# Router logits with the tokens' columns on the loaded side of TensorE, and VectorE reading them out of PSUM

## The chip, the cores and the metric

The kernel is one program on 1 core of one Trainium2 chip. The metric is the device time of the program in microseconds (us), as the median of repeated runs. The document also shows one profiled execution of the kernel, taken by the hardware profiler.

## The reference: what is computed

A transformer block over 4 sequences of 2048 tokens of width 256 (8192 tokens in all): a modulated layer norm, causal linear attention with 16 heads of width 16 and its output product, a gated residual sum, a second modulated layer norm, and a mixture of experts with 8 experts, of which each token takes 2. The part that the change touches is the router:

```python
logits = xf.astype(jnp.float32) @ w_router.T        # [8192, 256] @ [256, 8]
gates = jax.nn.softmax(logits, axis=-1)
topk_gates, topk_idx = jax.lax.top_k(gates, TOP_K)  # TOP_K = 2
expert_mask = jax.nn.one_hot(topk_idx, N_EXPERTS, dtype=jnp.int32).sum(axis=1)
position_in_expert = jnp.cumsum(expert_mask, axis=0) - 1
```

Everything is float32. The tokens' places with their experts come from a running count over all tokens, so group follows group in the routing.

## The kernel before, in words

The kernel has an attention phase and an expert phase. The attention phase goes over 64 tiles of 128 tokens, written as slots n. Four tiles make a group (16 groups), and q = n % 4 is the place of a slot in its group. In each slot every engine issues its own list of instructions in a fixed order, and the engines meet through semaphores. The loop is unrolled by 8 slots, so there are even groups (slots 0 to 3 of the eight) and odd groups (slots 4 to 7).

What stands in a slot on PE (TensorE), in its order: the scores of the tile (`scores`, L1269), which VectorE (DVE) then multiplies by the causal mask in two instructions (L919); what belongs to the next group's projections (`stage1_qk`, L1365, in q = 1 and 2; `stage1_v`, L1375, in q = 3; `stage1_transposes`, L1349, in q = 0); the transpositions of the tile before (`head_rows`, L1279); the products with the state (L1289, after the first half of DVE's mask) and the key rows (`key_rows`, L1295, after the second half); products within the tile (L1305); the transposed attention rows (L1330, after DVE's `An`, L935); the state (L1320, and L1315 in slot 0 of the eight alone); the output product (L1338); and last, in q = 0, the router's logits of the group two before (`logits`, L1417).

`stage1_qk` with m = 0, in q = 1, splits the activations into a high and a low part. Its last two matmuls wait for the low part `hT`, which GpSimd (POOL) makes in two instructions (L532) after ScalarE (ACT) has made the high part (L656); both of these hang on the transpositions of q = 0 (L1349) and not on the logits.

The logits now: `w_r` (256 x 32, of which 8 columns count) is the loaded side of PE, in two chunks `cc`, and the 128 token columns of `h2T` stream past it, once for each of the 4 tiles t. The four tiles go to four different bands of 32 output partitions of PJ[1] (`PJ[1][32 * t:32 * t + 32, 0:P]`). So the logits stand with the experts on the partitions. In the next slot (q = 1) ACT copies them to SBUF (`lgT`, L732), PE transposes them after its scores (`logit_rows`, L1424), ACT copies the result to `lg` (`take`, L699), after the masked queries for the next tile (L709), and DVE starts the routing (`choose`): `lmax` (L985) and `lp` (L987) are its first two steps, set between the small instructions ahead of `An`. In the tail, slot 63 has the logits of group 14 and slot 68 those of group 15.

The routing ends in q = 3 with L1053 (semaphore `route`), and GpSimd then sends the rows of the group to their experts with 8 indirect DMAs (L495). The expert phase begins when all rows are sent.

Of the kernel before, what the change touches and what calls it, by code (L numbers as in the profile page):

```python
# [17 lines left out]
ALU = mybir.AluOpType  # L18
ACT = mybir.ActivationFunctionType
AX_X = mybir.AxisListType.X  # L20

P = 128
D = 256
DC = D // P
# [10 lines left out]
GT = 4  # L35
# [3 lines left out]
E = 8  # L39
# [10 lines left out]
NR = 28  # L50


def adaln_block(nc, x, wqkv, wo, wr, wg, wd, c, wmod, out, xe, mod_rows):
    with ExitStack() as ctx:
        def sb(name, shape, dt=F32):
            return ctx.enter_context(nc.sbuf_tensor(name, shape, dt))

        def ps(name):
            return ctx.enter_context(nc.psum_tensor(name, [P, 512], F32))

        def sem(name):
            return ctx.enter_context(nc.semaphore(name))
# [11 lines left out]
        h2T = sb("h2T", [P, DC, GW])  # L74
# [7 lines left out]
        w_qkv = sb("w_qkv", [P, 2, DC, 3 * D], F32R)  # L82
        w_o = sb("w_o", [P, DC, D])
        w_r = sb("w_r", [P, DC, 32])
        lgT = sb("lgT", [P, P])
        w_g = sb("w_g", [P, 2, DC, F], F32R)
        cT = sb("cT", [P, DC, BATCH])
        cS = sb("cS", [P, DC, BATCH])
# [3 lines left out]
        ident = sb("ident", [P, P])  # L92
# [24 lines left out]
        nb2 = sb("nb2", [P, GT])  # L117
        den = sb("den", [P, H])
        rden = sb("rden", [P, H])
        lg = sb("lg", [P, GT, E])  # L120
        lmax = sb("lmax", [P, GT])
        lp = sb("lp", [P, GT, E])
        lp2 = sb("lp2", [P, GT, E])
# [8 lines left out]
        pick = sb("pick", [P, 2, GT, E])  # L132
# [46 lines left out]
        PJ = [ps("PJ0"), ps("PJ1")]  # L179
# [7 lines left out]
        lg_ps = PJ[1][:, P:2 * P].rearrange("p (t w) -> p t w", t=GT)  # L187
# [61 lines left out]
        h2t_full = sem("h2t_full")  # L249
        h2t_done = sem("h2t_done")  # L250
        wr_zero = sem("wr_zero")
        lgt_full = sem("lgt_full")
        lgt_done = sem("lgt_done")
        lg_full = sem("lg_full")
        taken = sem("taken")
        route = sem("route")
        gexp = sem("gexp")
        numbered = sem("numbered")
# [38 lines left out]
        def tile_ok(n):  # L297
            return 0 <= n < TILES
# [8 lines left out]
        def group_ok(n):  # L307
            return 0 <= n < GROUPS
# [310 lines left out]
        def _(act):  # L619
# [73 lines left out]
                for t in range(GT):  # L693
                    normalise(N1[:, t, :], t, L * GT + t, rs1, nb1, n1_ready)

            def take(dst, src, s_full, g):

                act.wait_ge(s_full, g + 1)
                act.activation(dst[:], src, ACT.Copy).then_inc(taken, 1)  # L699

            def next_tile_queries(T, q, gp, tp, n):

                q1, g1 = (q + 1) % 4, (gp if q < 3 else 1 - gp)
# [17 lines left out]
            def slot_(it, j, n):  # L721
                T = it * 8 + j
                G = it * 2 + j // 4
# [3 lines left out]
                stage1 = group_ok(nx)  # L727
                g, step = routing(n)
                routed = group_ok(g)
                if routed and step in ("first", "pick"):  # L730
                    act.wait_ge(lgt_full, g + 1)
                    act.activation(lgT[:], PJ[1][:, 0:P], ACT.Copy).then_inc(lgt_done, 1)  # L732
                if tile_ok(n + 1) and q != 3:
                    next_tile_queries(T, q, gp, tp, n)
                if routed and step in ("first", "pick"):
                    take(lg, lg_ps[:, :, 0:E], lg_full, g)
                def columns_out():
                    for cidx in range(DC):
                        act.wait_ge(h2t_full, 2 * g + cidx + 1)
# [73 lines left out]

            act.wait_ge(dve_setup, 2)
            run_slots(slot_, early)


# [51 lines left out]
        def _(dve):  # L869
# [102 lines left out]
            def wide(a):  # L972
                return a.unsqueeze(2).to_broadcast([P, GT, E])

            def done(ins):
                ins.then_inc(route, 1)

            def choose(g, k):

                if k == 0:  # L980
                    dve.wait_ge(taken, g + 1)
                else:
                    dve.wait_ge(route, NR * g + k)
                if k == 0:
                    done(dve.tensor_reduce(lmax[:], lg[:], AX_X, ALU.max))  # L985
                elif k == 1:
                    done(dve.tensor_tensor(lp[:], lg[:], wide(lmax[:]), ALU.subtract))  # L987
                elif k == 2:

                    done(dve.tensor_scalar(lp[:], lp[:], -104.0, None, ALU.max))  # L990
                elif k == 3:
                    done(dve.scalar_tensor_tensor(cand[:], lp[:], 0.0, revb, ALU.is_equal, ALU.mult))
                elif k == 4:
                    done(dve.tensor_reduce(rk[:, 0, :], cand[:], AX_X, ALU.max))
                elif k == 5:
                    done(dve.tensor_tensor(oh[:, 0], revb, wide(rk[:, 0, :]), ALU.is_equal))
                elif k == 6:
                    done(dve.scalar_tensor_tensor(lp2[:], oh[:, 0], -1.0e30, lp[:], ALU.mult, ALU.add))
                elif k == 7:
                    done(dve.tensor_reduce(m2[:], lp2[:], AX_X, ALU.max))  # L1000
                elif k == 8:
                    done(dve.tensor_tensor(cand[:], lp2[:], wide(m2[:]), ALU.is_equal))
                elif k == 9:
                    done(dve.tensor_tensor(cand[:], cand[:], revb, ALU.mult))
                elif k == 10:
                    done(dve.tensor_reduce(rk[:, 1, :], cand[:], AX_X, ALU.max))
                elif k == 11:
                    done(dve.tensor_tensor(oh[:, 1], revb, wide(rk[:, 1, :]), ALU.is_equal))
                elif k == 12:
                    done(dve.tensor_tensor(mask, oh[:, 0], oh[:, 1], ALU.add))  # L1010
# [218 lines left out]
        def _(pe):  # L1229
            mm = pe.matmul  # L1230
# [3 lines left out]
            for m in range(2 * DC):  # L1234
                for k in range(DC):
                    last = mm(MA[:, m * BATCH:(m + 1) * BATCH], wmod_sb[:, k, m * P:(m + 1) * P], cS[:, k, 0:BATCH],
                              start=(k == 0), stop=(k == DC - 1))
# [172 lines left out]
            def logits(g, gn, stage1):  # L1410

                if stage1:
                    pe.wait_ge(h_raw, 2 * (gn + 1) + 2)
                pe.wait_ge(h2t_done, 2 * g + 2)
                for cc in range(DC):
                    for t in range(GT):
                        last = mm(PJ[1][32 * t:32 * t + 32, 0:P], w_r[:, cc, :], h2T[:, cc, t * P:(t + 1) * P],  # L1417
                                  start=(cc == 0), stop=(cc == DC - 1), skip_group_check=True)
                last.then_inc(lgt_full, 1)

            def logit_rows(g):

                pe.wait_ge(lgt_done, g + 1)
                pe.transpose(PJ[1][:, P:2 * P], lgT[:], ident[:]).then_inc(lg_full, 1)  # L1424

            def positions(g, gn):

# [11 lines left out]
            def slot_(it, j, n):  # L1439
                T = it * 8 + j  # L1440
                G = it * 2 + j // 4
                gn, q, gp = n // 4, j % 4, (j // 4) % 2
                tp = j % 2
                stage1 = group_ok(gn + 1)
                g, step = routing(n)
                routed = group_ok(g)
                if tile_ok(n):
                    scores(T, q, gp, tp)
                if routed and step in ("first", "pick"):
                    logit_rows(g)  # L1450
                if n == TILES - 3:
                    second_columns()
                if routed and step == "columns" and n != TILES - 1:
                    h2_transposes(g, gn)
                if stage1:
                    if q == 1:
                        stage1_qk(G, 0)
                    elif q == 2:
                        stage1_qk(G, 2)
                    elif q == 3:  # L1460
                        stage1_v(G, 0)
                if routed and step == "place":
                    positions(g, gn)
                if tile_ok(n - 1):
                    head_rows(T)
                if tile_ok(n):
                    from_state(T, q, gp)
                if n == TILES - 1:
                    h2_transposes(g, gn)
                if stage1 and q == 0:  # L1470
                    stage1_transposes(G, gn)
                if tile_ok(n):
                    key_rows(T, q, gp)
                    from_tile(T, G, q, gp, tp, 0)
                if tile_ok(n - 1):
                    attention_columns(T)
                if tile_ok(n):
                    from_tile(T, G, q, gp, tp, 1)
                    add_to_state(T, q, gp, tp, j)
                if tile_ok(n - 1):  # L1480
                    out_product(T, n)
                if stage1:
                    if q == 1:
                        if group_ok(gn - 2):
                            pe.wait_ge(taken, G - 2 + 1)
                        stage1_qk(G, 1)
                    elif q == 2:
                        stage1_qk(G, 3)
                    elif q == 3:
                        if group_ok(gn - 2):  # L1490
                            pe.wait_ge(route, NR * (G - 2) + 15)
                        stage1_v(G, 1)
                if routed and step == "columns":
                    logits(g, gn, stage1)

            run_slots(slot_, early)


# [92 lines left out]
```

## Time and profile before

| | us |
|---|---|
| median of 3 runs | 863.83 |
| fastest and slowest run | 863.52, 989.26 |
| profiled execution, device time | 863.09 |
| profiled execution, span from first to last instruction | 861.1 |

The span is the time from the first to the last instruction; 2.0 us of the profiled execution lie around it. The attention phase takes the span's first 557 us or so, the rest of the routing and sending goes on to about 594 us, and the expert phase takes what is left. PE is matmul on TensorE and PEld its weight loads, which overlap it. A float32 matmul shows as two records, so 8 matmuls of the logits are 16 records; a transposition is one.

### The profile page before, as it was taken

Reading aid. Unit: us, or ns where it says so; the run is one execution under the profiler, and the core shown is the slowest. Engines: PE = TensorE matmul, PEld = TensorE weight load, DVE = VectorE, ACT = ScalarE, POOL = GpSimd, SP = SyncE. Lnnn points to the kernel's source line nnn. Section 1 sums busy time; section 2 is a strip of 40 time slices with the busy share of each in tenths; the row PEclk is TensorE's granted clock in tenths of the full one; section 3 lists DMA queues with packets and bytes.
Section 4 is the critical chain, followed back from the end, with each engine's and each line's share of the span. In section 5 each row is a group of like instructions: output and inputs, shape, how many; then the busy total and the mean of one; then the engine's idle time right before and its main releaser. Section 6 shows DMA issues by size and latency. Waiting matters only on the chain.

```text
span 861.1 us, 24360 instructions
## 1 busy us (share of the span) xinstructions
PE 790.2 (92%) x9388; PEld 647.2 (75%) x9388; DVE 585.6 (68%) x1753; ACT 488.7 (57%) x1001; POOL 472.5 (55%) x579
## 2 busy tenths in 40 slices
PE   5899999999999999999999999722999999999993
PEld 4676777777777777777777777511999999999993
DVE  4666677777776877867777767770566767767662
ACT  5656665766756756667657665421555555554541
POOL 2202345664664675665656645465356656656654
PEclk9999999999999999999999999955999999999997
DMA  5579913232332233323222212223466676677553
GB/s 195 175 229 284 310 19 125 84 91 100 84 114 90 86 111 95 83 97 71 66 86 64 52 50 58 48 78 120 102 155 130 135 167 133 146 158 156 122 91 37
DMA packets 71425, 99.00 MB, mean 115 GB/s; under 512 B 7810, under 2 KB 52866, under 8 KB 71320
## 3 DMA queue, kind: packets, MB, share of 16 engines
q1 hardware_dynamic: 38744, 53.93, 22.7%
q0 software_dynamic: 21760, 31.66, 16.9%
q10 hardware_dynamic: 10816, 11.96, 4.4%
q8 instruction: 71, 1.16, 0.6%
q14 instruction: 34, 0.28, 0.1%
HBM read 46.84 MB, written 63.36 MB: 128 GB/s over the span
## 4 chain that ended last, share of the span: by engine, by line
PE 73%; POOL 9%; issue 6%; ACT 6%; DVE 4%; DMA 2%; ACTq 0%; POOLq 0%; SPq 0%; DVEq 0%
PE SCW L1523 13%; PE PJ L1365 7%; PE SCW L1538 7%; PE MD L1538 6%; PE SCW L1305 6%; PE MD L1338 5%; PE SCW L1269 5%; PE PJ L1375 3%; PE SCW L1289 3%; POOL slot_rows L495 3%; PE MD L1279 3%; ACT N L671 2%; POOL rs L539 2%; POOL hT L532 2%; DVE Sm L919 2%
## 5 line engine op out<-in xcount | busy, mean ns | idle before, releaser
L495 POOL DMA_INDIRECT slot_rows<-Hrow,sloti x128 | 127.5, 996 | 141.4 <-PE SCW L1295 57.5
L919 DVE TENSOR_TENSOR Sm<-SCW,tri 128x1024 f32<-128x1024 f32 x128 | 150.8, 1220 | 71.5 <-PE SCW L1269 69.9
L601 POOL DMA_INDIRECT out<-EX,desti x80 | 128.2, 1602 | 31.8 <-issue 31.8
L1365 PE MATMUL PJ<-hT,w_qkv 128*128 128x512 f32 x384 | 109.8, 419 | 2.4 <-POOL hT L532 2.4
L1365 PEld LDWEIGHTS PJ<-hT,w_qkv 128*128 128x128 f32 x384 | 69.8, 190 | 25.5 <-issue 7.2
L671 ACT ACTIVATE N<-X,nb,rs 128x256 f32<-128x256 f32 x128 | 66.3, 591 | 27.4 <-POOL nb L541 27.4
L1305 PE MATMUL SCW<-Sm,VA 128*17 128x128 f32 x2048 | 80.6, 275 | 0.0
L667 ACT ACTIVATE EX<-PJ 128x512 f32<-128x512 f32 x64 | 37.9, 592 | 66.7 <-PE PJ L1365 66.7
L1269 PE MATMUL SCW<-QM,KT 32*128 32x256 f32 x1024 | 73.3, 400 | 0.8 <-ACT OTs L789 0.5
L1338 PE MATMUL MD<-w_og,ATs 128*128 128x256 f32 x256 | 72.4, 405 | 0.5 <-ACT ATs L778 0.5
L827 ACT ACTIVATE VA<-SCW 128x512 f32<-128x512 f32 x80 | 47.8, 598 | 41.0 <-PE SCW L1523 40.5
L539 POOL TENSOR_TENSOR rs<-vp,mhalf 128x4 f32<-128x4 f32 x32 | 39.5, 1235 | 55.1 <-DVE vp L960 54.9
L532 POOL TENSOR_TENSOR hT<-N,hT 128x512 fp32r<-128x512 f32 x30 | 37.7, 1278 | 48.8 <-ACT hT L656 48.8
L1523 PE MATMUL SCW<-KS,w_g 128*128 128x256 f32 x480 | 63.8, 290 | 0.0
L438 POOL TENSOR_TENSOR idle<-mhalf 128x1 f32<-128x1 f32 x96 | 20.9, 217 | 76.7 <-DVE EX L1204 52.1
L1523 PE MATMUL SCW<-VS,w_g 128*128 128x256 f32 x480 | 61.8, 285 | 0.0
L1305 PEld LDWEIGHTS SCW<-Sm,VA 128*17 128x17 f32 x2048 | 45.0, 96 | 21.3 <-issue 21.3
L1269 PEld LDWEIGHTS SCW<-QM,KT 32*128 32x128 f32 x1024 | 46.4, 184 | 19.2 <-issue 15.9
L1538 PE MATMUL MD<-w_qkv,hT 128*128 128x256 f32 x384 | 60.5, 282 | 0.0
L1538 PE MATMUL SCW<-w_qkv,QS 128*128 128x256 f32 x416 | 60.4, 282 | 0.0
L1523 PEld LDWEIGHTS SCW<-KS,w_g 128*128 128x128 f32 x480 | 60.1, 194 | 0.4 <-DVE KS L1168 0.4
L1523 PEld LDWEIGHTS SCW<-VS,w_g 128*128 128x128 f32 x480 | 58.2, 188 | 0.0
(189 smaller groups left out, 1767.1 us busy)
## 6 DMA issues: line engine op xcount, KB each, us to landing
Hrow<-slot_rows SPq DMA_DIRECT2D x32, 516.0 KB, 4.1
slot_rows<-erow ACTq DMA_DIRECT2D x1, 10400.0 KB, 46.6
X<-x SPq DMA_DIRECT2D x16, 512.0 KB, 5.6
out<-X SPq DMA_DIRECT2D x16, 512.0 KB, 2.9
Hrow<-mod_rows SPq DMA_DIRECT2D x16, 512.0 KB, 7.9
QT<-slot_rows SPq DMA_DIRECT2D x8, 516.0 KB, 3.7
slot_rows<-Hrow,sloti POOLq DMA_INDIRECT x128, 2.8
N<-wd SPq DMA_DIRECT2D x4, 512.0 KB, 4.2
```

What stands on the lines that cost most here:

```text
L495: pool.indirect_dma_start(xe, bass.IndirectOffsetOnAxis(sloti[:, par, k, t:t + 1], 0), Hrow[:, par, t, :], None, bounds_check=SLOTS - 1, o ...
L532: pool.tensor_tensor(hT[:, 1, cidx, :], hT_raw[:, cidx, :], hT[:, 0, cidx, :].bitcast(F32), ALU.subtract).then_inc(h_lo, 1)
L539: pool.tensor_tensor(rs[:], vp[:], mhalf[:], ALU.pow).then_inc(s_pow, 1)
L601: pool.indirect_dma_start(out, bass.IndirectOffsetOnAxis(desti[s % 2][:, a:a + 1], 0), Ys[s % 2][:, a, :], None, bounds_check=TOK - 1, oob ...
L671: act.activation(dst, X[:, bass.ds(xt, 1), :].rearrange("p a d -> p (a d)"), ACT.Identity, scale=rs[:, t:t + 1], bias=nb[:, t:t + 1]).then ...
L919: dve.tensor_tensor(o.rearrange("p c (k w) -> p c k w", k=2), SCW[:, 2 * pair:2 * pair + 2, :].rearrange("p k (c w) -> p c k w", c=DC), tr ...
L1269: last = mm(SCW[:, r, cc * 2 * P:(cc + 1) * 2 * P], KT[rows, gp, cc, q * P:(q + 1) * P], QM[rows, tp, :, cc, :], start=True, stop=True)
L1305: last = mm(OB[32 * a:32 * a + SW, part, cc, :], VA[:, gp, q, h, :], Sm[:, tp, h, :], start=False, stop=(part == 1), skip_group_check=True)
L1338: last = mm(MD[:, 0:D], ATs[:, cc, :], w_og[:, cc, :], start=(cc == 0), stop=(cc == DC - 1))
L1365: last = mm(PJ[m % 2][:], w_qkv[:, wp, cc, m * P:(m + 1) * P], hT[:, hp, cc, :], start=(cc + i == 0), stop=(cc == DC - 1 and i == len(SPLI ...
L1523: last = mm(SC[hh][:, (f % 2) * BW:(f % 2 + 1) * BW], w_g[:, wp, cc, f * P:(f + 1) * P], XT[par][:, xp, cc, :], start=(cc + i == 0), stop= ...
L1538: last = mm((MA, MD)[par][:, a * D:(a + 1) * D], hid[par][hp][:, f, a * P:(a + 1) * P], WD[k][wp][:, f, :], start=(f + i == 0), stop=(f == ...
```

## The change

The two sides of the router's matmuls are exchanged. The token columns of `h2T` (128 x 128) become the loaded side and `w_r` (32 columns) streams past them, so the logits come out with the tokens on the partitions, one block of 32 columns for each tile, in `lg_ps`. The copy `lgT`, PE's transposition `logit_rows` and the copy `lg` are gone with their semaphores. DVE's first two routing steps read `lg_ps` from PSUM. Before PE writes PJ[1] again (`stage1_qk(G, 1)`, end of the slot q = 1), it waits for DVE's second routing step and no longer for ACT's copy.

```diff
-                if routed and step in ("first", "pick"):
-                    act.wait_ge(lgt_full, g + 1)
-                    act.activation(lgT[:], PJ[1][:, 0:P], ACT.Copy).then_inc(lgt_done, 1)
                 if tile_ok(n + 1) and q != 3:
                     next_tile_queries(T, q, gp, tp, n)
-                if routed and step in ("first", "pick"):
-                    take(lg, lg_ps[:, :, 0:E], lg_full, g)
...
                 if k == 0:
-                    dve.wait_ge(taken, g + 1)
+                    dve.wait_ge(lg_full, g + 1)
                 else:
                     dve.wait_ge(route, NR * g + k)
                 if k == 0:
-                    done(dve.tensor_reduce(lmax[:], lg[:], AX_X, ALU.max))
+                    done(dve.tensor_reduce(lmax[:], lg_ps[:, :, 0:E], AX_X, ALU.max))
                 elif k == 1:
-                    done(dve.tensor_tensor(lp[:], lg[:], wide(lmax[:]), ALU.subtract))
+                    done(dve.tensor_tensor(lp[:], lg_ps[:, :, 0:E], wide(lmax[:]), ALU.subtract))
...
                 pe.wait_ge(h2t_done, 2 * g + 2)
-                for cc in range(DC):
-                    for t in range(GT):
-                        last = mm(PJ[1][32 * t:32 * t + 32, 0:P], w_r[:, cc, :], h2T[:, cc, t * P:(t + 1) * P],
+                for t in range(GT):
+                    for cc in range(DC):
+                        last = mm(lg_ps[:, t, :], h2T[:, cc, t * P:(t + 1) * P], w_r[:, cc, :],
                                   start=(cc == 0), stop=(cc == DC - 1), skip_group_check=True)
-                last.then_inc(lgt_full, 1)
-
-            def logit_rows(g):
-
-                pe.wait_ge(lgt_done, g + 1)
-                pe.transpose(PJ[1][:, P:2 * P], lgT[:], ident[:]).then_inc(lg_full, 1)
+                last.then_inc(lg_full, 1)
...
-                if routed and step in ("first", "pick"):
-                    logit_rows(g)
...
                         if group_ok(gn - 2):
-                            pe.wait_ge(taken, G - 2 + 1)
+                            pe.wait_ge(route, NR * (G - 2) + 2)
                         stage1_qk(G, 1)
```

## Rows read from the trace of the kernel before

**Rows 1.** The page: granted clock by fortieths of the span, and the chain that ended last.

```profile
PEclk9999999999999999999999999955999999999997
PE 73%; POOL 9%; issue 6%; ACT 6%; DVE 4%; DMA 2%; ACTq 0%; POOLq 0%; SPq 0%; DVEq 0%
```

**Rows 2.** The critical chain, 300 to 375 us: start, length, what.

```profile
368.77 0.57 PE PJ L1417 x16
```

**Rows 3.** The timeline of PE around the logits of an even group: start, length, merged records.

```profile
99.03 0.44 PE L1315 MATMUL SB<-Sbd,ident 128*128 128x68 f32 x2
...
99.66 1.13 PE L1338 MATMUL MD<-w_og,ATs 128*128 128x256 f32 x4
100.72 0.65 PE L1417 MATMUL PJ<-h2T,w_r 128*32 128x128 f32 x16
101.30 1.15 PE L1269 MATMUL SCW<-QM,KT 32*128 32x256 f32 x16
102.37 0.33 PE L1424 MATMUL PJ<-ident,lgT 128*128 128x128 f32 x1
102.46 1.63 PE L1365 MATMUL PJ<-hT,w_qkv 128*128 128x512 f32 x6
```

**Rows 4.** The same around the logits of the odd group after it, and the next even one.

```profile
133.59 0.64 PE L1417 MATMUL PJ<-h2T,w_r 128*32 128x128 f32 x16
...
135.32 1.17 PE L1365 MATMUL PJ<-hT,w_qkv 128*128 128x512 f32 x4
136.66 0.73 PE L1365 MATMUL PJ<-hT,w_qkv 128*128 128x512 f32 x2 [0.17 <-POOL hT L532]
...
167.54 0.64 PE L1417 MATMUL PJ<-h2T,w_r 128*32 128x128 f32 x16
```

**Rows 5.** The timeline of PE's weight loads after the scores of an even group.

```profile
373.04 0.20 PEld L1295 LDWEIGHTS SCW<-ident,KT 128*128 128x128 f32 x2 [0.17 <-DVE Sm L919]
```

**Rows 6.** The waits, 92 to 560 us: total, times, longest.

```profile
PE PJ L1432 <- ACT KT L668: 4.2, 12, 0.4
```

**Rows 7.** One line of the program's start: min/median/max ns, first and last start.

```profile
L1236 PE MATMUL SCW<-cS,Sm x16: 344/354/354, 6.3 to 9.5; 128*128 128x4 f32 x16
```

**Rows 8.** The timeline of PE: the same 8 transpositions at the start and later.

```profile
12.21 1.94 PE L1349 MATMUL PJ<-ident,N 128*128 128x128 f32 x8 [2.34 <-ACT N L671]
...
330.87 1.09 PE L1349 MATMUL PJ<-ident,N 128*128 128x128 f32 x8
331.79 0.38 PE L1295 MATMUL SCW<-ident,KT 128*128 128x128 f32 x2
```

**Rows 9.** The timeline of PE, bfloat16 loads of 128x128.

```profile
321.92 0.22 PE L1434 MATMUL PJ<-masks,ones 128*128 128x24 bf16 x3
322.00 0.18 PE L1436 MATMUL PJ<-masks,ones 128*128 128x32 bf16 x1
```

**Rows 10.** The timeline of DVE, small instructions with operands in PSUM and in SBUF.

```profile
322.88 0.18 DVE L1023 TENSOR_TENSOR pbase<-PJ,base 128x32 f32<-128x32 f32 x1
...
339.44 0.13 DVE L987 TENSOR_TENSOR lp<-lg,lmax 128x32 f32<-128x32 f32 x1
```

**Rows 11.** The timeline around the logits of group 14.

```profile
557.17 0.64 PE L1417 MATMUL PJ<-h2T,w_r 128*32 128x128 f32 x16
...
560.49 0.17 DVE L928 TENSOR_SCALAR den<-MD 128x16 f32<-128x16 f32 x1
```

**Rows 12.** The timeline around the logits of group 15 and the last sends.

```profile
572.27 1.08 PE L1417 MATMUL PJ<-h2T,w_r 128*32 128x128 f32 x16 [0.87 <-ACT h2T L745]
...
574.49 0.19 DVE L985 TENSOR_REDUCE lmax<-lg 128x4 f32<-128x32 f32 x1 [0.20 <-ACT lg L699]
...
580.09 0.17 DVE L1053 TENSOR_TENSOR Hrow<-gk,esum 128x8 f32<-128x8 f32 x1
...
582.16 0.19 POOL L454 TENSOR_TENSOR idle<-mhalf 128x1 f32<-128x1 f32 x1 [0.17 <-POOL Hrow L464]
```

**Rows 13.** Busy time by window: PE, PEld, DVE, ACT, POOL, granted clock, DMA share, GB/s.

```profile
564.00:574.00 10.00, 3.61 (x30) 2.55 (x30) 6.40 (x33) 3.90 (x7) 6.40 (x8) 0.50 0.24 70
```

More of the change, by code:

```diff
@@ L84, in adaln_block @@
         w_r = sb("w_r", [P, DC, 32])
-        lgT = sb("lgT", [P, P])
         w_g = sb("w_g", [P, 2, DC, F], F32R)
@@ L119, in adaln_block @@
         rden = sb("rden", [P, H])
-        lg = sb("lg", [P, GT, E])
         lmax = sb("lmax", [P, GT])
@@ L251, in adaln_block @@
         wr_zero = sem("wr_zero")
-        lgt_full = sem("lgt_full")
-        lgt_done = sem("lgt_done")
         lg_full = sem("lg_full")
-        taken = sem("taken")
         route = sem("route")
@@ L694, in ln1_norm @@
                     normalise(N1[:, t, :], t, L * GT + t, rs1, nb1, n1_ready)
-            def take(dst, src, s_full, g):
-                act.wait_ge(s_full, g + 1)
-                act.activation(dst[:], src, ACT.Copy).then_inc(taken, 1)
             def next_tile_queries(T, q, gp, tp, n):
```

## The prediction, on record before the changed kernel was timed

> **What bounds the kernel now.** I read the page first. The chain that ended last runs through TensorE (PE) for 73% of the span, and the granted clock stands at its full level from end to end but for two fortieths between the phases [rows 1]. So work added to PE counts unless something covers it. Then the chain of waits inside the attention phase: the 16 records of the logits stand on it themselves, 0.57 us [rows 2]. Then PE's timeline around them, in an even and in an odd group. In an even group the records follow each other without a gap: logits at 100.72, scores at 101.30, the transposition at 102.37, the projection at 102.46 [rows 3]. In an odd group there is one gap: the six projection records take 1.63 us from the first one's start in the even group [rows 3], and 136.66 + 0.73 - 135.32 = 2.07 in the odd one, where the last two wait for GpSimd's `hT` [rows 4]. So an odd group has 2.07 - 1.63 = 0.44 us of slack for anything that delays PE between the transpositions of q = 0, on which `hT` hangs, and this place. Even groups have none, because L1315 (starting 99.03, [rows 3]) delays PE there and not in odd ones.
>
> Does a delay of PE go through to the end? The distance from even to odd logits is 133.59 - 100.72 = 32.87, from odd to even 167.54 - 133.59 = 33.95 [rows 3, 4]. The difference, 1.08, is close to the 0.44 of the `hT` gap and the 0.44 of L1315's two records [rows 3], 0.88 together. A gap and an added matmul both lengthen the period by about what they are, so I take one to one.
>
> **The change, part by part.**
>
> *Removed on PE.* The old logits hold PE from 100.72 to 101.30, 0.58 us for 16 records, 0.036 each, because four products with 32 loaded columns run beside each other in four bands [rows 3]. The transposition holds it from 102.37 to 102.46, 0.09 us [rows 3].
>
> *Added on PE.* 8 matmuls with 128x128 float32 loaded and 32 columns streamed, 16 records, one after another, as each load fills all columns. The trace has nearly this form once: L1236, 128x128 loads and 4 columns, 16 records that start between 6.3 and 9.5 us, 3.2 / 15 = 0.213 apiece [rows 7]. At what clock? The 8 transpositions behind them took 1.94 us, and the same line later takes 1.09 [rows 8], a ratio of 1.8; the old logits show the like, 1.08 us where the clock is granted at 0.50, its level of 1.2 GHz, and 0.65 at the full 2.4 GHz [rows 3, 12, 13]. So L1236 ran at the low level, and at the full one a record that is bound by its load should take half, 0.107. Transpositions with the same loads start 0.115 apart at full clock, (331.79 - 330.87) / 8 [rows 8]. Bounds: above, L1338 with the same loads and 256 streamed columns, (100.72 - 99.66) / 4 = 0.265 [rows 3]; below, bfloat16 loads of the same shape, (322.00 - 321.92) / 3 = 0.027 [rows 9]. I take 0.115, the nearest row at full clock: 16 x 0.115 = 1.84 us. The new logits cost PE 1.84 - 0.58 = 1.26 us more for each group.
>
> The Trainium skill, "TensorE: Matmul & The Clock Gate", section "Back-to-back issue gap", puts a matmul of 1 to 64 streamed columns at about 25 ns; by that 16 records would be 0.4 us and the change a gain on PE. Its section "LDWEIGHTS" makes the loaded columns the price, 107 ns for 128, and its section on weight-path modes keeps the fast load from FP32. By that 16 records are 1.71 us and the sum is 8 x 1.13 + 6 x 0.60 = 12.6, 876. The row of L1236 speaks for the second and the bfloat16 row shows what the exception is worth.
>
> *Where it lies.* The logits end the slot q = 0; the scores, DVE's mask and all of the next slot stand behind them. Even groups (n = 8, 16, ... 56; seven) and group 13 (n = 60, with no projection and no `hT` behind it) pay 1.26. Of the 0.09 I give back nothing there: behind the scores PE's loads for the key rows already wait for DVE's second mask half [rows 5], which starts from the scores; PE would only wait there longer. Odd groups with `hT` (n = 12, 20, ... 52; six) pay 1.26 - 0.09 - 0.44 = 0.73. Sum: 8 x 1.26 + 6 x 0.73 = 10.1 + 4.4 = 14.5 us.
>
> *Tail.* Group 14: its logits start at 557.17, and what is late next is DVE with eight wide instructions, which reads PE's next result at 560.49 [rows 11]. PE would be done with logits and four transpositions at 557.17 + 1.84 + 0.5 = 559.5: nothing. Group 15 runs at the low clock [rows 13]: 15 x 0.213 and one record's own 0.35 [rows 7], 3.54 us from 572.27, so `lmax` at 575.8 in place of 574.49, 1.3 later. The routing, which ended at 580.09 + 0.17, then ends at 580.26 + 1.3 = 581.6, and GpSimd, still sending group 14, comes to its wait for it at 582.16 [rows 12]: nothing, with 0.6 to spare. If that cover were gone it would cost at most 1.3 us.
>
> *Removed on ACT.* Two copies a group and their waits. ACT's next task is the masked queries, needed a whole slot later; PE hardly waits for them. Nothing.
>
> *DVE.* Two reads move from SBUF to PSUM. `lp` takes 0.13 now, and a like instruction out of PSUM 0.18 [rows 10]; two times 0.05 ahead of `An`, at most 0.1 x 14 = 1.4 us if DVE is last, and no gain, since nothing in it gets shorter. I take 0, since PE has products of the tile between the key rows and `An`. `choose` starts on PE's semaphore and no longer on ACT's; it was not late, as it stands behind both masks in DVE's queue.
>
> *The new wait* of PE ahead of `stage1_qk(G, 1)`: DVE's second routing step comes before `An`, and PE has passed the wait for `An` by then. Nothing is queued behind it that wasn't.
>
> The profiled execution took 863.09 us, 0.74 below the median. 863.09 + 14.5 = 877.6, or 878.3 beside the median; I say 878.
>
> **The rivals.**
>
> A. *Load and stream in series.* If a record's 32 columns don't run beside the next load, a record is 0.107 and, at most, 32/256 of L1338's 0.265, 0.033: 0.140. 16 are 2.24, the addition 1.66 (even) and 1.13 (odd): 8 x 1.66 + 6 x 1.13 = 20.1, 883 us. For: L1338 takes over twice a load. Against: L1236 shows no more than one load, though with 4 columns it could hardly show more. At L1338's full 0.265 16 records are 4.24: 8 x 3.66 + 6 x 3.13 = 48 us, 911; I give that end 2 in 100.
>
> B. *The load is cheap* (the other side: not slower). With the bfloat16 rows' 0.027 [rows 9], 16 records are 0.43, 0.15 less than now; with nothing gained where DVE or `hT` is last, 14 x 0.15 = 2.1 us faster, 861. It decides for "faster" from 0.58 / 16 = 0.036 for a record downwards. The Trainium skill's figure of 25 ns ("Back-to-back issue gap", cited above) is this rival. Against: L1236 and the transpositions, both over 0.1 with full float32 loads.
>
> C. *More slack than `hT`'s.* PE waits 12 times 0.35 us ahead of the positions in q = 3 for ACT, which hangs on GpSimd and DVE [rows 6]. If that chain doesn't start from PE's own delayed slot, it swallows 12 x 0.35 = 4.2 us: 863.1 + 14.5 - 4.2 = 873.4. With the transposition's 0.09 and a shorter record it reaches down to 870. Against: GpSimd's part of it stands in its queue behind sends that wait for PE in the same slot.
>
> D. *The clock.* The new logits keep the array thinly used for 1.8 us. Two slices with the low level in them stand between the phases, 2 x 21.5 us long [rows 1]; as the old logits took 1.08 there and 0.65 at the full level, as much work in the attention phase would take up to 43 x (1 - 0.65 / 1.08) = 17 us longer: 863.1 + 14.5 + 17 = 895. For: the clock did fall behind the sparse tail. Against: it held through every group so far.
>
> **How the numbers follow.** Forecast 54 in 100, A 20 (2 of them at the far end), C 13, B 9, D 3, and 1 for other things. The range leaves out B, D and A's far end and takes in C down to 867 and A up to 886, which also holds records of up to 0.15 (16 x 0.035 = 0.56 more than the forecast's, 14 times: 7.8). Two per cent, about what a measurement of this kernel can tell from no change, is 17.3 us, a limit of 881.1: above it are D, A's larger part and the forecast's upper edge (a record of 0.13 and more), 25 together; faster by over 2% would need more than the whole of what PE gives up, 14 x 0.67 = 9.4 us: 1. Within 2%: 74.
>
> **What the profile after would show.** L1417's successor with 128x128 loads, 16 records a group, in 1.7 to 2.1 us from its first start to the scores (0.43 under B, 2.2 and more under A); no `hT` gap in odd groups; 34.1 us from even to odd and 34.7 from odd to even; the granted clock unchanged; `lmax` still right behind `den`; the expert phase the same length. Wrong would make me: a record under 0.04; a gap on PE that shrinks elsewhere in the group (L1432) by what the logits gained in length; or a tail in which GpSimd waits for group 15's routing.

## The result and the profile after

The changed kernel took 876.05 us (median of 4 runs), the kernel before 867.33 in all its runs by then; the ratio is 1.0117, with an interval of 1.0073 to 1.0161. One of the four runs of each kernel was far slower than its others (910.56 and 989.26 us) and does not enter the ratio. At 865 us, about what the kernel before takes in the later comparisons, the ratio means 10 us more: less than two per cent, and clear of no change. The span of the profiled execution is 872.7 us, 11.6 more than before.

The page of the changed kernel: granted clock, and the chain that ended last.

```profile
PEclk9999999999999999999999999965999999999997
...
PE 80%; POOL 6%; issue 5%; ACT 4%; DVE 3%; DMA 1%; ACTq 0%; POOLq 0%; DVEq 0%; SPq 0%
```

The clock stands as before [rows 1], and PE's part of the chain has grown from 73 to 80%. The line numbers have moved: the logits are L1402 now, the scores L1254, the projections L1350, the output product L1323. The timeline of PE, around the logits of an even group:

```profile
168.06 1.13 PE L1323 MATMUL MD<-w_og,ATs 128*128 128x256 f32 x4
169.03 1.87 PE L1402 MATMUL PJ<-w_r,h2T 128*128 128x32 f32 x16
170.83 1.15 PE L1254 MATMUL SCW<-QM,KT 32*128 32x256 f32 x16
171.90 1.66 PE L1350 MATMUL PJ<-hT,w_qkv 128*128 128x512 f32 x6
```

and of the odd group before it:

```profile
134.43 1.87 PE L1402 MATMUL PJ<-w_r,h2T 128*128 128x32 f32 x16
...
137.30 1.66 PE L1350 MATMUL PJ<-hT,w_qkv 128*128 128x512 f32 x6
```

Read the starts. The logits hold PE from 169.03 to 170.83, 1.80 us for 16 records, 0.112 each. But they begin 0.09 us nearer to the output product than before (0.97 behind its start, and 1.06 in [rows 3]), so from the output product's start to the scores it is 2.77 us now and was 101.30 - 99.66 = 1.64: 1.13 us more. In the odd group the six projection records stand in one row of 1.66 us with no wait: the gap that GpSimd's `hT` made [rows 4] has been filled. The logits of group 14 now start at 568.08, 10.9 later than before [rows 11]; so nearly all of the loss lies in the attention phase.

The same kernel's tail, groups 14 (first two rows) and 15:

```profile
568.08 1.97 PE L1402 MATMUL PJ<-w_r,h2T 128*128 128x32 f32 x16
...
571.39 0.17 DVE L913 TENSOR_SCALAR den<-MD 128x16 f32<-128x16 f32 x1
...
583.48 3.62 PE L1402 MATMUL PJ<-w_r,h2T 128*128 128x32 f32 x16 [0.87 <-ACT h2T L730]
...
587.15 0.19 DVE L970 TENSOR_REDUCE lmax<-PJ 128x4 f32<-128x32 f32 x1 [1.65 <-PE PJ L1402]
...
592.89 0.17 DVE L1038 TENSOR_TENSOR Hrow<-gk,esum 128x8 f32<-128x8 f32 x1
...
593.36 0.19 POOL L449 TENSOR_TENSOR idle<-mhalf 128x1 f32<-128x1 f32 x1 [0.17 <-POOL Hrow L459]
```

`den` of group 14 comes 3.3 us behind the logits' start, as before (560.49 - 557.17, [rows 11]): the wide instructions of VectorE cover the longer logits. In group 15 `lmax` comes 3.67 us behind them and came 2.22 behind them [rows 12], and the routing ends at 593.06, 0.3 us before GpSimd gets to it.

There is a second, smaller difference. It concerns two instructions outside the router. GpSimd's `rs` (L534; L539 before) raises the second norm's variances to the power -1/2 in q = 2; its two operands have 4 elements in a partition. (The same line does it again for the first norm right behind.) VectorE's `phi` (L938; L953 before) makes the feature map of the keys `KT`, 128x512. The timeline of the changed kernel at two places, the same point of two even groups:

```profile
253.87 1.61 POOL L534 TENSOR_TENSOR rs<-vp,mhalf 128x4 f32<-128x4 f32 x1
253.90 0.70 DVE L938 SCALAR_TENSOR_TENSOR KT<-KT,EX 128x512 f32<-128x512 f32 x1
...
322.54 1.05 POOL L534 TENSOR_TENSOR rs<-vp,mhalf 128x4 f32<-128x4 f32 x1
322.56 0.75 DVE L938 SCALAR_TENSOR_TENSOR KT<-KT,EX 128x512 f32<-128x512 f32 x1
```

`rs` takes 1.61 us in one and 1.05 in the other, though VectorE's `phi` starts right behind it in both. In the trace of before it is about 1.6 in every group of the middle of the run. `phi` itself takes 0.75 us where `rs` is short and 0.70 where it is long. In the changed kernel two of these groups (322.54 and 390.72) have the short one, and there the way from the group's logits to the next is 33.57 and 33.58 us, where it is 34.07 to 34.09 in the even groups with the long one. The first and the last even group stand outside this: 33.96 with a `rs` of 1.02, and 33.54 with one of 1.55.

### The profile page after: what moved, and what is told of

Its sections match the earlier page's. It is cut to its first block, busy times and chain, and to the rows that moved or that the text cites. A ratio compares the mean times of both kernels' runs of the same rounds, so it can differ in the third digit from the quotient of the medians.

```text
span 872.7 us, 24296 instructions
## 1 busy us (share of the span) xinstructions
PE 807.0 (92%) x9372; PEld 673.3 (77%) x9372; DVE 583.5 (67%) x1753; ACT 482.4 (55%) x969; POOL 470.0 (54%) x579
## 4 chain that ended last, share of the span: by engine, by line
PE 80%; POOL 6%; issue 5%; ACT 4%; DVE 3%; DMA 1%; ACTq 0%; POOLq 0%; DVEq 0%; SPq 0%
PE SCW L1501 13%; PE PJ L1350 9%; PE SCW L1290 7%; PE SCW L1516 7%; PE MD L1323 7%; PE SCW L1254 6%; PE MD L1516 6%; PE PJ L1360 4%; PE SCW L1274 3%; PE MD L1264 3%; POOL slot_rows L490 3%; PE PJ L1402 3%; PE SCW L1315 2%; PE SCW L1280 2%; PE PJ L1487 2%
## 5 line engine op out<-in xcount | busy, mean ns | idle before, releaser
L1350 PE MATMUL PJ<-hT,w_qkv 128*128 128x512 f32 x384 | 108.5, 418 | 1.4 <-POOL hT L527 1.4
L1350 PEld LDWEIGHTS PJ<-hT,w_qkv 128*128 128x128 f32 x384 | 69.5, 188 | 26.7 <-issue 11.5
L1254 PE MATMUL SCW<-QM,KT 32*128 32x256 f32 x1024 | 73.3, 400 | 0.8 <-ACT OTs L774 0.5
L1323 PE MATMUL MD<-w_og,ATs 128*128 128x256 f32 x256 | 73.2, 409 | 0.5 <-ACT ATs L763 0.5
L534 POOL TENSOR_TENSOR rs<-vp,mhalf 128x4 f32<-128x4 f32 x32 | 38.4, 1200 | 56.1 <-DVE vp L945 55.6
L1254 PEld LDWEIGHTS SCW<-QM,KT 32*128 32x128 f32 x1024 | 46.4, 184 | 17.1 <-issue 13.2
```

Source lines behind the costliest of these rows:

```text
L534: pool.tensor_tensor(rs[:], vp[:], mhalf[:], ALU.pow).then_inc(s_pow, 1)
L1254: last = mm(SCW[:, r, cc * 2 * P:(cc + 1) * 2 * P], KT[rows, gp, cc, q * P:(q + 1) * P], QM[rows, tp, :, cc, :], start=True, stop=True)
L1323: last = mm(MD[:, 0:D], ATs[:, cc, :], w_og[:, cc, :], start=(cc == 0), stop=(cc == DC - 1))
L1350: last = mm(PJ[m % 2][:], w_qkv[:, wp, cc, m * P:(m + 1) * P], hT[:, hp, cc, :], start=(cc + i == 0), stop=(cc == DC - 1 and i == len(SPLI ...
```

## The experiments

The ratios are to the kernel before, run on the same chip in the same comparison.

**reads_psum: the reads out of PSUM and the moved waits alone.** The kernel before without ACT's second copy, `lg`:

```diff
-                if routed and step in ("first", "pick"):
-                    take(lg, lg_ps[:, :, 0:E], lg_full, g)
...
-                    dve.wait_ge(taken, g + 1)
+                    dve.wait_ge(lg_full, g + 1)
...
-                    done(dve.tensor_reduce(lmax[:], lg[:], AX_X, ALU.max))
+                    done(dve.tensor_reduce(lmax[:], lg_ps[:, :, 0:E], AX_X, ALU.max))
-                    done(dve.tensor_tensor(lp[:], lg[:], wide(lmax[:]), ALU.subtract))
+                    done(dve.tensor_tensor(lp[:], lg_ps[:, :, 0:E], wide(lmax[:]), ALU.subtract))
...
-                            pe.wait_ge(taken, G - 2 + 1)
+                            pe.wait_ge(route, NR * (G - 2) + 2)
```

> The kernel before, with one part of the change alone: the logits still come out with the experts on the partitions, are copied to lgT and transposed by PE, but the copy lg is left out and VectorE's first two routing steps read the transposition's result in PSUM. Theory (all of the change's cost is PE's longer logits): within 1 us of the kernel before, since lmax and lp take as long out of PSUM (0.18 and 0.13 us in the changed kernel's trace) and ACT's copy was on no path. Rival (the moved reads and waits cost or save something themselves): at least 1.4 us apart from the kernel before, 14 times 0.1 us.

Measured: ratio 1.0018 (0.999 to 1.0045). The moved reads and the moved waits, PE's new one among them, cost nothing that can be told. The changed kernel's line of `lp` says why (min, median and max in ns):

```profile
L972 DVE TENSOR_TENSOR lp<-PJ,lmax x16: 127/128/192, 106.1 to 587.4; 128x32 f32<-128x32 f32 x16
```

It takes 0.128 us out of PSUM, and took 0.13 out of SBUF [rows 10].

**columns_8: the streamed side.**

```diff
-                        last = mm(lg_ps[:, t, :], h2T[:, cc, t * P:(t + 1) * P], w_r[:, cc, :],
+                        last = mm(lg_ps[:, t, 0:E], h2T[:, cc, t * P:(t + 1) * P], w_r[:, cc, 0:E],
```

> The changed kernel, with 8 columns of w_r streamed past the loaded token columns and not 32 (the other 24 are zeros that nobody reads). Theory (a record is held up by its load of 128 columns alone): logits stay at 1.75 to 1.80 us from their first start to the scores, span 872.7 within 1 us. Rival (load and stream stand in series): 24 columns fewer are 24/256 of L1338's 0.265 us, 0.025 for a record, 0.4 us for a group, 14 groups 5.6 us, span 867.

Measured: ratio 1.0137 (1.0086 to 1.0188), span 872.0. The timeline of PE in this kernel:

```profile
168.76 1.85 PE L1402 MATMUL PJ<-w_r,h2T 128*128 128x8 f32 x16
170.54 1.15 PE L1254 MATMUL SCW<-QM,KT 32*128 32x256 f32 x16
```

1.78 us for 16 records, 0.111 each, against 0.112 with 32 columns. The time is within the noise of the changed kernel's. Load and stream don't stand in series, as rival A had it.

**logits_twice: does a microsecond on PE go through to the end?**

```diff
+                for again in range(2):
                     for t in range(GT):
                         for cc in range(DC):
                             last = mm(lg_ps[:, t, :], h2T[:, cc, t * P:(t + 1) * P], w_r[:, cc, :],
...
```

> The changed kernel, with the 8 logits' matmuls of each group issued twice into the same place; the second pass starts the sum anew, so the result is the same. Theory (each microsecond of PE goes to the end one to one, the slack of hT being used up): 1.8 us for 14 groups, 25.2; 0.7 in group 14, where VectorE covered 1.1; and about 3 us in group 15 at the low clock, where 0.4 of the cover is left: span 901.6. Rival (there is more slack in a group, ahead of the positions in q = 3): 4.2 us less, 897 or below.

Measured: ratio 1.0656 (1.0613 to 1.0699), span 925.9, 53 us over the changed kernel where 29 were expected, and a mean granted clock of 0.942 for 0.971. Neither theory had that. The windows of this kernel, 39 and 36 us from one group's logits on, and the 3 us around the end of the first of these logits (length; busy time of PE, PEld, DVE, ACT, POOL; granted clock; DMA share; GB/s), and the timeline of PE at the start of the two:

```profile
249.00:288.00 39.00, 38.59 (x471) 29.87 (x470) 25.19 (x80) 20.94 (x47) 20.31 (x28) 0.91 0.25 80
288.00:324.00 36.00, 35.59 (x471) 27.63 (x470) 24.98 (x80) 21.53 (x48) 20.31 (x28) 1.00 0.27 90
...
253.00:256.00 3.00, 3.00 (x20) 2.04 (x20) 0.58 (x1) 0.00 (x0) 0.00 (x0) 0.50 0.00 0
```

```profile
249.37 3.96 PE L1403 MATMUL PJ<-w_r,h2T 128*128 128x32 f32 x32
253.26 2.09 PE L1254 MATMUL SCW<-QM,KT 32*128 32x256 f32 x16
255.29 2.93 PE L1350 MATMUL PJ<-hT,w_qkv 128*128 128x512 f32 x6
...
288.33 3.65 PE L1403 MATMUL PJ<-w_r,h2T 128*128 128x32 f32 x32
291.92 1.15 PE L1254 MATMUL SCW<-QM,KT 32*128 32x256 f32 x16
```

Behind the doubled logits the scores take 2.09 us in the first group and 1.15 in the second. In the first group the granted clock stood at 0.50 there, its low level (1.2 GHz). It had fallen before the doubled logits ended: they hold PE for 3.89 us, and for 3.59 in the second group. It rose to the full level again within the group. Of the first thirteen groups nine have such a stretch, by their length beside that in dense_pass below, and four have none.

**dense_pass: the same time on PE, with 128 columns streamed.** In front of the changed kernel's logits:

```diff
+                for t in range(GT):
+                    for cc in range(DC):
+                        mm(PJ[1][:, 0:P].rearrange("p (a w) -> p a w", a=4), h2T[:, cc, t * P:(t + 1) * P],
+                           w_r[:, cc, :].unsqueeze(1).to_broadcast([P, 4, 32]),
+                           start=(cc == 0), stop=(cc == DC - 1), skip_group_check=True)
```

> The changed kernel, with a first pass over the same 8 loads in front of the logits that streams 128 columns (w_r's 32 four times) into a part of PJ[1] that nobody reads, in place of the thin second pass of the kernel with the logits twice. It asks what the lower granted clock in that kernel came from (mean clock 0.942, span 925.9). Theory (the clock fell because PE stood on loads with few columns streamed for 3.6 us on end): a record of the dense pass takes 0.14 to 0.16 us, 2.2 to 2.6 us for a group and 31 to 36 us in all, with 3 to 4 in the tail, and the clock stays at its full level in the attention phase: mean near 0.97, span 907 to 913. Rival (any 2 us more of matmuls between loads there bring it down): low stretches behind the logits as in the kernel with the logits twice, mean 0.94, span 930 or more.

Measured, in two runs: ratio 1.0498 (1.044 to 1.0555), span 905.3, mean clock 0.967. The span is 1.7 us below the theory's. The windows of logits_twice first, then of this kernel, and its timeline of PE:

```profile
92.00:600.00 508.00, 501.26 (x6372) 388.63 (x6370) 336.25 (x1062) 285.08 (x628) 264.17 (x363) 0.96 0.27 78
```

```profile
92.00:580.00 488.00, 481.63 (x6362) 375.97 (x6361) 334.01 (x1057) 284.61 (x627) 263.01 (x362) 1.00 0.29 82
```

```profile
172.43 1.95 PE L1402 MATMUL PJ<-w_r,h2T 128*128 128x128 f32 x16
174.22 1.87 PE L1407 MATMUL PJ<-w_r,h2T 128*128 128x32 f32 x16
176.02 1.15 PE L1254 MATMUL SCW<-QM,KT 32*128 32x256 f32 x16
```

Two things follow. The dense pass takes 174.22 - 172.43 = 1.79 us: 0.112 for a record with 128 streamed columns, as with 32 and with 8. The expected 0.14 to 0.16 was wrong; the load of 128 columns alone sets the pace up to there. And PE is held for as long as in logits_twice, 1.79 + 1.80 us in a group, but the clock stays at the full level throughout 92 to 580 us. So of the 925.9 - 905.3 = 20.6 us between the two kernels most are the clock's: 17.0 are there when group 14's logits start (611.89 against 594.90). The rest comes in the tail, and was not traced. A mean of 0.96 over 508 us gives 4%, or 20 us, as the most that the clock can have cost there. The added pass itself costs 905.3 - 872.7 = 32.6 us, where 14 times 1.79 (25.1) and the tail's 3.7 make 28.8. By the starts of the logits, 26.8 are there when group 14's start. Of these 1.4 more than a pass lie in group 13, and 0.5 in a group where the changed kernel has the short `rs` and this one the long. The other 5.8 lie in the tail, 2.1 more than reckoned, also not traced.

**bands_32 and bands_8: four loads of 32 columns beside each other.**

```diff
                 for t in range(GT):
                     for cc in range(DC):
-                        last = mm(lg_ps[:, t, :], h2T[:, cc, t * P:(t + 1) * P], w_r[:, cc, :],
-                                  start=(cc == 0), stop=(cc == DC - 1), skip_group_check=True)
+                        for s in range(4):
+                            last = mm(lg_ps[32 * s:32 * s + 32, t, :],
+                                      h2T[:, cc, t * P + 32 * s:t * P + 32 * s + 32], w_r[:, cc, :],
+                                      start=(cc == 0), stop=(cc == DC - 1), skip_group_check=True)
```

bands_8 streams `w_r[:, cc, 0:E]`, into `lg_ps[32 * s:32 * s + 32, t, 0:E]`.

> The changed kernel, with each load of 128 token columns split into four of 32, for the four bands of 32 output partitions, so that four products run beside each other as in the kernel before: 32 matmuls, 64 records. Theory (the price is 128 loaded columns in one row; four bands load beside each other): 64 records at the pace of L1320's (32 loaded, 34 streamed, 16 records in 0.26 us) are 1.06 us; the addition over the kernel before is 0.48 in the eight groups without a gap and nothing in the six with hT's, 1.5 to 4 us in all, span 863 to 866. Rival (records are issued no faster than about 0.03 us each): 64 are 1.9 us, no gain over the changed kernel, 872 or more.

> The kernel with the token columns loaded in four bands of 32 (64 records in 0.72 us), with 8 columns of w_r streamed and not 32. Theory (with loads of 32 columns beside each other neither load nor stream holds a record, and what is left is the pace at which records are issued, 0.011 us): 0.70 to 0.76 us from the first start to the scores, span 864.4 within 1. Rival (the stream of 32 columns is part of the pace): 0.6 us or less, 0.1 us less for 8 groups, span 863.5, not to be told apart by its time but by the trace.

Measured: bands_32 1.0015 (0.9989 to 1.004), span 864.4; bands_8 1.0026 (1.0006 to 1.0047), span 864.1. The timeline of PE in bands_32, an odd group:

```profile
134.79 0.76 PE L1403 MATMUL PJ<-w_r,h2T 128*32 128x32 f32 x64
135.51 1.15 PE L1254 MATMUL SCW<-QM,KT 32*128 32x256 f32 x16
136.58 2.01 PE L1350 MATMUL PJ<-hT,w_qkv 128*128 128x512 f32 x6
```

64 records take 0.72 us, 0.011 each, less than the 1.06 expected, and less than half of the 0.028 that a quarter of 0.112 would give, if loads of 32 columns stood in a row as well; in bands_8 the merged row of 64 lasts 0.72 for 0.76, and the scores start 0.70 us behind it for 0.72, so the stream matters little here either. The projections take 2.01 us again: `hT`'s gap is back. The same products, with the same side loaded as in the changed kernel and with every other part of the change in place, cost 1.08 us less on PE, and with that nearly all of the 10 us is gone: the two kernels with bands are 0.15 and 0.26% above the kernel before. That shows the cause: it was the serial loads of 128 columns, not which side is loaded, and not the reads, copies and waits that go with it.

**phi_later: VectorE's order in q = 2, on the kernel before.**

```diff
-                if stage1 and q in (1, 2):
+                if stage1 and q == 1:
                     phi(G, 2 * (q - 1), npar)
                 between()
                 if q == 2 and group_ok(gn + 2):
                     ln_tail(st1, mv1, vp1, nm1, ag1, vpe1, G + 3)
+                if stage1 and q == 2:
+                    phi(G, 2 * (q - 1), npar)
                 between()
```

> The kernel before, with one order on VectorE changed and nothing of the router's: in q = 2 the small statistics of the first norm (ln_tail) come ahead of phi for KT. In both kernels GpSimd's rs (two operands of 4 elements) takes 1.61 us where VectorE's phi starts 0.01 to 0.03 us behind it, and 1.05 in two of the changed kernel's groups, whose distance to the next logits is then 0.5 us shorter. Theory (the two engines are in each other's way at the start, and 1.61 is the price): with phi some 0.7 us later rs takes 1.05 in all groups, 11 times 0.5 us, span 855 to 857. Rival (GpSimd is held up whenever VectorE's wide instruction falls anywhere on its rs, or phi, now later, is late for ACT): rs stays near 1.6, span 861 to 864.

Measured: ratio 0.9952 (0.9925 to 0.9979), faster by half a per cent. The timeline of this kernel in one group:

```profile
247.37 1.06 POOL L539 TENSOR_TENSOR rs<-vp,mhalf 128x4 f32<-128x4 f32 x1
247.39 0.37 DVE L957 BATCH_NORM_AGGREGATE mv<-st 128x2 f32<-128x6 f32 x4
...
247.94 0.69 DVE L953 SCALAR_TENSOR_TENSOR KT<-KT,EX 128x512 f32<-128x512 f32 x1
```

What starts with `rs` now is the small statistics instruction (L957), and `phi` starts within `rs`, 0.57 us behind its start; `rs` takes 1.06 and `phi` 0.69. `rs` is short so in all groups of the middle but the one near 512 us, and group 14's logits start at 551.10, 6.1 earlier than before [rows 11]. The profiled span, 862.6, doesn't show the gain: this execution's expert phase was some 7 us longer. So the theory's sign and its place hold; its size in the measured time is 4 us for the 5.5 expected.

The edit also brings the first norm's statistics forward, so it does not by itself say that the gain is `rs`'s. But PE's wait ahead of the positions in q = 3, which hangs on `KT`, all but goes. The waits of the kernel before are [rows 6]; here are those of the changed kernel and of phi_later:

```profile
PE PJ L1412 <- ACT KT L663: 3.6, 10, 0.4
```

```profile
PE PJ L1434 <- ACT KT L668: 0.4, 1, 0.4
```

And six groups of five kernels whose order on VectorE is untouched have the short `rs` by themselves: reads_psum at 183 us, columns_8 at 254 and 424, dense_pass at 407, bands_32 at 251, bands_8 at 252. In each `rs` takes 1.05 or 1.06 us, `phi` 0.74 or 0.75 where it takes 0.68 to 0.72 beside a long `rs`, and the way to the next logits is 0.3 to 0.5 us shorter than in the groups like it.

**changed_phi_later, bands_32_phi_later: both edits together.** They add the phi_later diff to the changed kernel and to bands_32.

> The changed kernel with VectorE's phi for KT behind the statistics in q = 2, as in phi_later. Theory (the two are independent: PE's longer logits cost about 1.1 us in each group without hT's gap wherever rs ends): rs takes 1.05 in all groups where it took 1.6 (nine of them), 0.5 us each, logits of group 14 at 568.1 - 4.5 = 563.5, and the ratio to the kernel before about 1.008. Rival (with rs early, something else in the group is last and takes the longer logits in): logits of group 14 at 561 or earlier, ratio 1.005 or less.

> The kernel with the token columns loaded in four bands of 32 and VectorE's phi for KT behind the statistics in q = 2. Theory: logits of group 14 5 to 6 us earlier than in the bands kernel (558.1), at 552 to 553, ratio to the kernel before 0.995 to 0.998, beside 0.9952 for the later phi alone. Rival (with rs 0.55 us shorter, PE's 0.05 us more for a group and ACT's two copies fewer weigh more than before): ratio 0.993 or less, or 1.000 and more.

Measured: 1.008 (1.0053 to 1.0107) and 1.0001 (0.9981 to 1.002), on another chip, where the kernel before took 880.64 us, 16 more than elsewhere. `rs` is short, but group 14's logits start at 581.94 and 573.33 us, where 563.5 and 552 to 553 were expected; that the first ratio is the expected one therefore confirms nothing. The waits of changed_phi_later, 92 to 560 us (total, times, longest), have one that these two kernels show and no trace of the other chips has, and PE's state products (L1307) halt beside it:

```profile
ACT ATs L763 <- remote: 25.7, 12, 2.2
...
PE SB L1307 <- issue: 7.9, 23, 0.5
```

Both halts lie in q = 2, where the shorter `rs` would give its gain. These two runs decide nothing of it. The last ones are the same two kernels on yet another chip, with the kernel before beside them.

> The kernel before once more, for its trace beside the two that follow. In the last comparison all kernels, the one before among them, took about 16 us longer than elsewhere (880.6 against 865), and the traces show a stall of about 1.2 us on PE in the state's products of q = 2 in every group. If that belongs to the chip, this kernel shows it too where the others do; if it belongs to the later phi, it doesn't, and the time is 863 to 867.

> The changed kernel with VectorE's later phi, a second time. If the chip is like the first ones: ratio to the kernel before 1.005 to 1.010 (1.0117 and 1.0137 less the 0.0048 of phi_later), logits of group 14 at 563 to 564. If PE stalls in q = 2 as in the last comparison: 1.008 again.

> The kernel with the four bands and VectorE's later phi, a second time. If the chip is like the first ones: ratio 0.995 to 0.998. If PE stalls in q = 2, a wait that hides what the shorter rs would give: 1.000 again.

Measured: before_again 1.0007 (0.9972 to 1.0042) at 865.28 us, without that wait; changed_phi_again 1.0063 (1.0034 to 1.0092), group 14's logits at 563.07, 5.0 earlier than in the changed kernel; bands_phi_again 0.9954 (0.9927 to 0.9982), 861.53 us against 865.05, span 858.0. Within the noise the two edits add up: 1.0117 to 1.0137 less 0.0048 gives 1.007 to 1.009, beside the 1.0063. The four bands with the later `phi` beat the kernel before and the changed one. They are not to be told from the later `phi` alone (0.9952), so the gain is the later `phi`'s. What halts PE on the other chip stays open. before_again ran on a chip where the halt is missing, so it was not shown that the kernel before halts on the other one, only that it is 16 us longer there.

## Why the prediction was right

It said 878 us, 867 to 886; measured were 876.05, and 10 us more than before for the 14.5 forecast (11.6 between the two profiled spans). The mechanism is the forecast one. The sum was too large by 3 to 4.5 us, and the paragraphs below say where; that the time itself is only 2 us off is in part because the kernel before came out above its 863.83 in the later runs.

*PE's record.* Right mechanism: the load of 128 columns sets the pace, at 0.112 us where 0.115 was taken from the transpositions and 0.107 from L1236. columns_8 and dense_pass show it with 8 and 128 columns. The addition was 1.13 us for a group, not 1.26: 0.04 of the difference is the pace, and the rest is that the first logits record starts 0.09 us nearer to the output product. 14 groups make 1.8 us of the forecast's excess.

*Where it lies.* Right in the main: the distance from even to odd logits was to be 34.1 us and is 134.43 - 100.47 = 33.96; from odd to even 34.7, and it is 169.03 - 134.43 = 34.60. `hT`'s gap went as said. The even group that the prediction read is not like the others, though: its distance was 32.87, and in the later even groups but the last it was 33.02 to 33.16, and is 34.07 to 34.09 with the long `rs`. So a later even group with the long `rs` pays 0.9 to 1.0 us for the 1.26. A part is the transposition's 0.09, which was given no value there: the scores start 1.22 us later behind the logits, the projections only 1.13 (171.90 - 169.03, and 102.46 - 100.72 in [rows 3]). The six odd groups pay 0.62 to 0.68 each for the 0.73.

*More slack (rival C).* The waits ahead of the positions did shrink, from 4.2 to 3.6 us and from 12 to 10 times, but not because PE's delay was swallowed: they are gone in the two groups where `rs` came out short, and are 0.35 us as before in the others. Two times 0.5 us are 1.0 of the excess. phi_later shows what these waits hang on: with the short `rs` nearly everywhere they fall to 0.4 us in all. The attention phase up to the first logits was 0.25 us shorter in the profiled execution (100.72 - 100.47). 14.5 - 1.8 - 1.0 - 0.25 = 11.4; group 14's logits are 568.08 - 557.17 = 10.9 later. The other 0.5 is a difference: beside 1.13 each, and the two short `rs`, the seven even groups grew by 0.9 less, and the other seven by 0.4 more than 1.13 - 0.09 - 0.44 = 0.60 each for the odd ones and 1.13 for group 13.

*Tail.* Right: the longer logits of group 14 are hidden by VectorE, those of group 15 by GpSimd's sends, with 0.3 us to spare for the 0.6 reckoned. `lmax` came 1.45 us later behind group 15's logits, for the 1.3 reckoned.

*ACT, DVE and the new wait.* Taken at nothing, and reads_psum shows nothing. The bound of 1.4 us on the reads was drawn from L1023, 0.18 us with an operand in PSUM [rows 10]; `lp` has the same shape and takes 0.128 out of PSUM, so PSUM alone is not what makes L1023 slower. What does was not looked for.

*The clock (rival D).* It did not fall in the changed kernel. It fell in logits_twice, with twice the length, and not in dense_pass, which is as long. Rival D priced a fall in the attention phase at up to 17 us, and logits_twice lost 17.0 there. That they agree is luck: the 43 us at the low level were taken from two slices between the phases, which have nothing to do with the groups.

*The cheap load (rival B)* is refuted for float32 loads of 128 columns: with 8, 32 and 128 columns streamed a record takes 0.111, 0.112 and 0.112 us. With bands of 32 loaded columns it takes 0.011. The Trainium skill, "TensorE: Matmul & The Clock Gate", section "Back-to-back issue gap", gives its 25 ns for a matmul taken by itself, and says that in a stream of loads and matmuls both set the spacing; the prediction left that out, and none of the three streams meets the 25 ns. The same page's section "LDWEIGHTS" comes to 107 ns for 128 columns, and these runs agree with it to within 6 ns.

## What to carry to other kernels

A record of a float32 matmul with 128 loaded columns cost PE its load here, 0.11 us, whether 8 or 128 columns were streamed. Before turning a product round to save a transposition and copies, count the loads that stand in a row, and see whether narrow bands can stand beside each other. Two copies a group and their handshakes, off the critical path, were worth nothing that could be measured here. Where a tiny instruction on GpSimd takes half as long again in some groups, see which instruction of VectorE starts with it: moving that one gained 4 us here, and no form of the router gained anything.

## What the runs showed of the hardware that was not expected

- PE is held for 3.6 us a group in both logits_twice and dense_pass, with the same loads. The granted clock fell in the first, where all 32 records stream 32 columns (0.96 over 92 to 600 us), and stayed full in the second, where the first 16 stream 128 (1.00 over 92 to 580 us).
- An instruction of 4 elements on GpSimd takes 1.61 or 1.05 us, and in the changed kernel's two rows above the start of VectorE's wide instruction behind it differs by no more than 0.01 us (0.03 and 0.02). With that instruction 0.57 us behind it is 1.06. Where GpSimd's is short, VectorE's is 0.05 us longer. That the two engines share something at that moment, and that one of them goes first, is argued from this, not shown: a kernel in which `rs` meets nothing at all was not run.
- `lp` is as fast out of PSUM as out of SBUF, 0.128 us for 128x32.
